# Score matmuls issued one head pair ahead, and the gate product moved from GpSimd to VectorE, in a retention block with FFN on eight Trainium2 cores

## The reference

```python
xn = layernorm(x)
# retention, 16 heads of 64
Q, K, V = xn @ Wq + bq, xn @ Wk + bk, xn @ Wv + bv      # split in heads
retained = ((Q @ K.T) / 8 * mask) @ V                   # mask[i, j] = 0.99**(i-j) for i >= j, else 0
normed = layernorm(retained) * gamma + beta             # over all 1024 features
s = (normed * sigmoid(xn @ Wg + bg)) @ Wo + bo
# feed-forward, 4096 wide
g = silu(gelu(xn @ w1 + b1) @ w2 + b2)
out = x + s * g
```

## Time and profile before

| quantity | value |
|---|---|
| three timed runs | 1761.42, 1877.56, 1886.75 us (median 1877.56) |
| the profiled execution's own time | 1759.84 us |
| span of its slowest core (core 3) | 1758.1 us |
| spans of the eight cores | 1728.0 to 1758.1 us |
| TensorE matmul busy in the span | 1359.8 us (77%) |
| VectorE, ScalarE, GpSimd busy | 469.7, 285.6, 146.4 us |

### The profile page before, as it was taken

One profiled execution on the slowest core, in us unless ns is written; L12 is line 12 of the kernel. 1 busy time (PEld: TensorE's weight loads), 2 busy tenths in 40 slices (PEclk: granted clock), 3 DMA queues, 4 the chain that ended last, 5 costly groups with the idle time before them and its releaser, 6 DMA issues.

```text
span 1758.1 us, 21259 instructions; the slowest of 8 cores (1728.0 to 1758.1 us)
## 1 busy us (share of the span) xinstructions
PE 1359.8 (77%) x7594; PEld 713.8 (41%) x7594; DVE 469.7 (27%) x1196; ACT 285.6 (16%) x594; POOL 146.4 (8%) x144
## 2 busy tenths in 40 slices
PE   0499966876287776886877868866599999999994
PEld 0144323533134323443343233432356666666662
DVE  0774011334044234233442342334001100111011
ACT  0021210110010110202101102011212222222221
POOL 0000000001000101001000010011002211221122
PEclk9988776887569677697686787976789999999997
DMA  8331034999700000001000000024502102110120
GB/s 154 107 113 44 1 72 84 124 116 118 110 1 24 25 1 25 25 0 48 1 25 25 1 4 22 1 96 156 212 4 72 49 25 72 73 48 32 65 73 36
DMA packets 15901, 100.42 MB, mean 57 GB/s; under 512 B 3253, under 2 KB 3638, under 8 KB 11830
## 3 DMA queue, kind: packets, MB, share of 16 engines
q0 software_dynamic: 6144, 44.06, 14.4%
q1 hardware_dynamic: 9510, 46.62, 8.2%
q10 hardware_dynamic: 144, 8.39, 1.3%
HBM read 109.56 MB, written 33.55 MB: 81 GB/s over the span
## 4 chain that ended last, share of the span: by engine, by line
PE 68%; DVE 12%; DMA 8%; issue 6%; ACT 3%; POOL 2%; DVEq 1%; SPq 0%; ACTq 0%; POOLq 0%
PE pY L1065 13%; PE pH L1041 9%; PE pPJ L555 7%; PE pM L867 6%; PE pPJ L517 4%; PE pS L790 4%; PE pPJ L534 3%; PE pPJ L592 3%; DMA s_scr<-WB 3%; PE pRT L642 2%; PE pRT L656 2%; PE pM L895 2%; PE pLATE L714 2%; DVE WB L627 2%; DMA WB<-w2b 2%
## 5 line engine op out<-in xcount | busy, mean ns | idle before, releaser
L1065 PE MATMUL pY<-WB,hT 128*128 128x512 bf16 x1024 | 226.6, 382 | 16.7 <-DMA WB<-w2b 16.7
L1041 PE MATMUL pH<-xnT,WB 128*128 128x256 bf16 x2048 | 227.5, 273 | 11.7 <-ACT hT L1051 10.7
L1041 PEld LDWEIGHTS pH<-xnT,WB 128*128 128x128 bf16 x2048 | 199.1, 98 | 41.6 <-issue 17.0
L790 PE MATMUL pS<-WB 128*128 128x512 bf16 x256 | 106.8, 540 | 122.3 <-POOL WB L780 66.3
L1065 PEld LDWEIGHTS pY<-WB,hT 128*128 128x128 bf16 x1024 | 100.9, 99 | 136.5 <-issue 20.8
L1095 DVE SCALAR_TENSOR_TENSOR xg<-pY,xg 128x1024 f32<-128x1024 f32 x16 | 19.6, 1225 | 471.6 <-ACT xg L1092 429.6
L1051 ACT ACTIVATE hT<-pH,b1Ts 128x256 bf16<-128x256 f32 x256 | 99.4, 479 | 226.8 <-PE pH L1041 226.8
L555 PE MATMUL pPJ<-xnT,WB 128*128 128x256 bf16 x1024 | 117.9, 276 | 12.3 <-DVE WB L546 12.3
L555 PEld LDWEIGHTS pPJ<-xnT,WB 128*128 128x128 bf16 x1024 | 93.7, 99 | 38.2 <-issue 16.3
L790 PEld LDWEIGHTS pS<-WB 128*128 128x128 bf16 x256 | 28.1, 116 | 194.4 <-issue 187.4
L867 PE MATMUL pM<-WB 128*128 128x512 bf16 x384 | 103.8, 436 | 0.0
(11 more groups left out here) (135 smaller groups left out, 1387.0 us busy)
## 6 DMA issues: line engine op xcount, KB each, us to landing
xg<-xpre SPq DMA_DIRECT2D x12, 1024.0 KB, 6.2
xg<-xseg SPq DMA_DIRECT2D x8, 1024.0 KB, 5.8
w1b<-w POOLq DMA_DIRECT2D x1, 8192.0 KB, 105.1
w2b<-w POOLq DMA_DIRECT2D x1, 8192.0 KB, 180.5
s_scr<-WB POOLq DMA_DIRECT2D x16, 512.0 KB, 3.0
xg<-xseg SPq DMA_DIRECT2D x16, 512.0 KB, 4.8
sld<-s_scr SPq DMA_DIRECT2D x16, 512.0 KB, 3.4
out<-sld POOLq DMA_DIRECT2D x16, 512.0 KB, 3.0
```

The source lines that it names most:

```text
L790: A("tensor", lambda e, it=it, dt=dt, ns=ns: e.matmul(pS[:, :], AsS[:, GRP * dt + 128 * it:GRP * dt + 128 * it + 128], WoS(1024 * dt + 512 ...
L1041: A("tensor", lambda e, dht=dht, dm=dm, sub=sub, pH=pH, gc=gc: e.matmul(pH[:, 256 * sub:256 * sub + 256], w1S(4096 * dm + 128 * dht, 128), ...
L1065: A("tensor", lambda e, lt=lt, dht=dht, ns=ns, it=it, pY=pY, half=half: e.matmul(pY[:, 512 * ns:512 * ns + 512], hT[:, 256 * lt + 128 * it ...
```

## The change

In `stageM2` the loop body is split in two functions. `m2_jb(hp)` issues the score matmuls and masks of a pair, `m2_ret(hp)` the matmuls that use them, the copy of `pRT` and the state's update. They are called as `m2_jb(0)`, and then for each pair `m2_jb(hp+1)` ahead of `m2_ret(hp)`. As two pairs' masked scores are alive at a time, the odd pairs get four tiles of their own, which lie in `xnb`; each mask of an odd pair also writes the token `b.xnb`, and each matmul on it reads that token. In `stageL` the product with the gate is issued on VectorE.

```diff
-                for hp in range(NP):
+                PmO = [xnb[:, 0:256], xnb[:, 256:512],
+                       xnb[:, 512:640], xnb[:, 640:768]]
+
+                def m2_jb(hp):
                     if hp % 2 == 0:
                         jb0b, jb0t = pSCB, "p.SCB"
                         jb1b, jb1t, jb1c = pSCA, "p.SCA", 256
+                        pm, pmt, extw = Pm, "b.Pm", []
                     else:
                         jb0b, jb0t = pLATE, "p.LATE"
                         jb1b, jb1t, jb1c = pS, "p.S", 0
+                        pm, pmt, extw = PmO, "b.PmX", ["b.xnb"]
...
-                          reads=[jb0t, "c.mask"], writes=["b.Pm0%d" % hh])
...
+                          reads=[jb0t, "c.mask"],
+                          writes=["%s0%d" % (pmt, hh)] + extw)
...
+                def m2_ret(hp):
+                    pm, pmt = (Pm, "b.Pm") if hp % 2 == 0 else (PmO, "b.PmX")
+                    extr = [] if hp % 2 == 0 else ["b.xnb"]
...
-                          reads=["b.V", "b.Pm0%d" % hh], writes=["p.RT"])
...
+                          reads=["b.V", "%s0%d" % (pmt, hh)] + extr,
+                          writes=["p.RT"])
...
+                m2_jb(0)
+                for hp in range(NP):
+                    if hp + 1 < NP:
+                        m2_jb(hp + 1)
+                    m2_ret(hp)
...
-                    A("gpsimd", lambda e, dt=dt, tA_=tA_: e.tensor_tensor(
+                    A("vector", lambda e, dt=dt, tA_=tA_: e.tensor_tensor(
                         AsS[:, GRP * dt:GRP * dt + GRP], tA_[:, :],
                         GtS[:, GRP * dt:GRP * dt + GRP], ALU.mult),
```

More of the change, by code:

```diff
@@ L626, in stageM2 @@
                           reads=["b.Ks", "b.Qs"], writes=[jb1t])
-                        A("vector", lambda e, hh=hh, jb0ap=jb0ap: e.tensor_tensor(
-                            Pm[hh][:, 0:256], jb0ap, maskS[:, 0:256],
+                        A("vector", lambda e, hh=hh, jb0ap=jb0ap, pm=pm: e.tensor_tensor(
+                            pm[hh][:, 0:256], jb0ap, maskS[:, 0:256],
                             ALU.mult),
-                          reads=[jb0t, "c.mask"], writes=["b.Pm0%d" % hh])
-                        A("vector", lambda e, hh=hh, jb1ap=jb1ap: e.tensor_tensor(
-                            Pm[2 + hh][:, 0:128], jb1ap, maskS[:, 0:128],
+                          reads=[jb0t, "c.mask"],
+                          writes=["%s0%d" % (pmt, hh)] + extw)
+                        A("vector", lambda e, hh=hh, jb1ap=jb1ap, pm=pm: e.tensor_tensor(
+                            pm[2 + hh][:, 0:128], jb1ap, maskS[:, 0:128],
                             ALU.mult),
[L634 to L638, removed]
+                          reads=[jb1t, "c.mask"],
+                          writes=["%s1%d" % (pmt, hh)] + extw)
+                def m2_ret(hp):
+                    pm, pmt = (Pm, "b.Pm") if hp % 2 == 0 else (PmO, "b.PmX")
+                    extr = [] if hp % 2 == 0 else ["b.xnb"]
                     for hh in range(2):
@@ L641, in stageM2 @@
                         ro = 64 * hh
[L642 removed]
+                        A("tensor", lambda e, h=h, ro=ro, hh=hh, pm=pm: e.matmul(
                             pRT[ro:ro + 64, 0:256] if ro == 0 else pRT[64:128, 0:256],
                             VS[:, 64 * h:64 * h + 64],
[L645 removed]
+                            pm[hh][:, 0:256],
                             start=True, stop=False, skip_group_check=True,
                             tile_position=(0, ro)),
[L648 to L649 removed]
+                          reads=["b.V", "%s0%d" % (pmt, hh)] + extr,
+                          writes=["p.RT"])
+                        A("tensor", lambda e, h=h, ro=ro, hh=hh, pm=pm: e.matmul(
                             pRT[ro:ro + 64, 128:256] if ro == 0 else pRT[64:128, 128:256],
                             VS[:, 1024 + 64 * h:1024 + 64 * h + 64],
[L652 removed]
+                            pm[2 + hh][:, 0:128],
                             start=False, stop=False, skip_group_check=True,
                             tile_position=(0, ro)),
[L655 removed]
+                          reads=["b.V", "%s1%d" % (pmt, hh)] + extr,
+                          writes=["p.RT"])
                         A("tensor", lambda e, h=h, ro=ro, hp=hp: e.matmul(
@@ L669, in stageM2 @@
                         for it in range(2):
-                            A("tensor", lambda e, h=h, ro=ro, it=it, hp=hp, g=g: e.matmul(
+                            A("tensor", lambda e, h=h, ro=ro, it=it, hp=hp: e.matmul(
                                 pSU[ro:ro + 64, 64 * hp:64 * hp + 64] if ro == 0
@@ L677, in stageM2 @@
                               reads=["b.Ku", "b.V"], writes=["p.SU"])
+                m2_jb(0)
[3 more added lines that the diff above has]
+                    m2_ret(hp)
+                if dbg and g == 0:
+                    A("sync", lambda e: e.dma_start(
+                        out=d_Pm[:, :], in_=Pm[0][:, 0:256]),
+                      reads=["b.Pm00"], writes=["d.out"], dma=True)
                 A("vector", lambda e: e.scalar_tensor_tensor(
```

## The result

| quantity | before | after |
|---|---|---|
| median of ten runs each | 1762.19 us (1756.65 to 1890.03) | 1787.58 us (1769.47 to 1865.47) |
| the profiled execution's own time | 1759.84 us | 1783.96 us |
| span of its slowest core (core 3) | 1758.1 us | 1782.4 us |
| spans of the eight cores | 1728.0 to 1758.1 us | 1758.7 to 1782.4 us |

The ratio of after to before is 1.0143, with the interval 1.0107 to 1.0179: about 25 us slower, and under the 2% line. With no change in the program some runs of either kernel lie 4 to 7% above the rest, four of the ten of before (1844 to 1890 us, two of them among the three runs shown ahead of the prediction) and two of the ten of after, and the ratio leaves these out.

What follows compares the result with a forecast made beforehand. TensorE's waits bound it: in stageL for VectorE's chain, in stageM2 for a mask. 22.5 + 3.1 = 25.6 us more gives 1785 us at the profiled level, 1903.2 us at the median's; range 1768 to 1925 us.

Steps and rivals of the forecast that it cites:

- The level: Whole kernel: 25.6 us added to the three timed runs' median of 1877.56 us, giving 1903.2 us.
- The sum: Whole kernel: 22.5 us from stageL plus 3.1 us from stageM2, 25.6 us more on 1759.84 us.
- Part 1: StageL's product on VectorE: a tile takes 1.92 us instead of 1.39, costing 22.5 us over groups 1 to 7.
- Part 2: StageM2's scores one pair ahead: 5.3 us lost less 2.2 us saved, net +3.1 us.
- The term of the odd pairs: StageM2: token b.xnb delays the second mask of each odd pair by 0.19 us, 5.3 us in all.
- The full-clock saving: StageM2 at full clock: the second head's matmuls no longer wait for masks, 0.23 us a pair, 2.2 us saved.
- Group 0's cover: Group 0's stageL: ScalarE's copy waits 36.71 us for a store behind the w2b transfer, absorbing all that group loses.
- Rival 1: StageM2: the other pair fills the second head's score wait, gaining 32.8 us; total -12.5 us, 1747 us; chance 5%.
- Rival 2: StageL: GpSimd sets the pace and the product gets cheaper, 0.42 for 0.72 us; about 1760 us; chance 6%.
- Rival 3: VectorE operations never overlap, 0.53 us apart throughout; stageL 4.6 us more a group, +30 us, 1790 us; chance 10%.
- Rival 4: Gate projection after stageL's longer pass: clock returns later, 25 us more, together +51 us, 1811 us; chance 12%.

Runs made afterwards that it cites:

- the first experiment: Product on VectorE alone, on the kernel before: 1762.73 us, ratio 1.0127 (1.0059 to 1.0194).
- the fastest kernel: Against the kernel before: scores ahead, token per tile, bank per head, interleaved product on VectorE, retained matmuls alternating between heads: 1632.3 us, ratio 0.9333.

## Why the prediction was near in the sum and wrong in the time

**The level (wrong).** The prediction says: "Both parts are stretches of waiting between engines, so I add the same sum to the median: 1877.56 + 25.6 = 1903.2 us." This is the step that failed. The sum was made against the profiled execution at 1759.84 us, and 1785 us is what came (1783.96 profiled, 1787.58 as a median). Three runs, of which two lay 6% up, were taken as the centre of the kernel's time, though the profiled execution and one of the three stood together at 1760. The median of ten runs is 1762.19. The range held both levels and so held the result.

**The sum (near, by offsets).** +25.6 us against +25 by the medians and +24.1 between the profiled executions.

- *Part 1, 22.5 us.* The path was right. The distances 0.53, 0.53, 0.53, 0.33 came as 0.53, 0.53, 0.51, 0.35, and the tile as 1.91 instead of 1.92 us. The stretch came as 15.61 us on average (15.50 to 15.85), for 15.60 in the sum. StageL as a whole lost 27.3 us: 109.3 - 86.1 = 23.2 in that stretch, 3.1 in the passes behind it, whose length depends on when the clock rises, and 1.0 around the broadcasts. In group 5 two of the three later passes ran at full clock before (1.89 us each from the first start to the last end, 3.57 at half clock), and after it was one. The product alone agrees, with 193 us of stageL for 164 and a total some 22 us longer.
- *Part 2, +3.1 us.* The term of the odd pairs was right: 3.52 against 3.34 us, and 6 us less once the shared token was gone, for 5.3 in the sum. Three of the four odd pairs stand inside the loop and the fourth at its start. What was missed is the rest of the start (0.68 us a group less that fourth 0.2) and the end (0.39), together about 6 us. I costed a pair in the steady state and never walked the first and the last one. The full-clock saving of 2.2 us didn't show: the full-clock time at the start of the stage now goes into the longer wait there. This part cost 11.8 us, not 3.1, so the size of this term was wrong too, by more than the sum shows.
- *Offsets.* StageS and stageM1 gave back 10.8 us, and the head start of core 3 in phase 0 another 3.3. StageS holds the same instructions, and in group 4 it took 13.40 us at a mean clock of 0.70 before and 11.90 us at 0.87 after. These are the two stretches, of before and then of after, in the columns of the earlier trace rows. It isn't a property of the new order: with the product alone, core 1 has 91.7 us of stageS and core 5 86.0. In stageM1 it is one stretch at half clock fewer in group 6 (41.75 to 39.64 us) and two fewer in group 7 (39.73 to 36.42), less 0.8 us in group 1. I had no term for this, and no run here shows what sets it. So that +24.1 us came so near to +25.6 is in good part luck: without these offsets the two parts cost 39 us on this core, of which the sum had two thirds.

```profile
859.40:872.80 13.40, 11.11 (x37) 3.31 (x33) 6.47 (x21) 3.21 (x9) 0.00 (x0) 0.70 0.01 1
```

```profile
871.40:883.30 11.90, 8.73 (x37) 2.89 (x34) 6.41 (x21) 3.18 (x9) 0.00 (x0) 0.87 0.01 2
```

- *Group 0's cover (right).* w2b took as long as before (180.3 us after its issue, 180.5 before), and the store's wait shrank. That the transfer is fixed held to 3 us only, since its issue moved.

**The rivals.** Rival 1, the overlap, needs the wait ahead of L620 gone; it is 39.9 us, and it goes when each head has a bank of its own. Then the order brings 46 us in the pairs (161 to 115, a part of it by the clock), more than the 32.8 us that I gave the wait. Rival 2, that GpSimd sets the pace, fell with the first experiment. Rival 3 (0.53 us throughout) fell with the 0.35 and 0.33 us in the rows. Of what the Trainium skill says in "VectorE: DVE Perf Modes", section "The DRAIN you can't avoid", the statement that a semaphore costs nothing extra doesn't hold here: the wait did cost 0.2 us for each operation. The other one, that the next operation doesn't start until the pipe is empty, the prediction cited without its limit: the same section adds that an operation which isn't held starts earlier, and the 0.33 us agree with that. Rival 4, a later clock, didn't come; the gate projection took 7.10 us at 1.00 in group 3, and sums to 50.4 us against 50.8.

## What to carry to other kernels

Work out an operation's cost by whether it waits for the one just ahead on its engine: moved onto a chain, a faster operation can cost more than a slower one on an idle engine, and interleaving two chains takes the cost away. When work is issued ahead to fill a wait, check in the engine's order that it stands in front of the waiting instruction; if it doesn't, find what the wait protects (here a bank shared by two heads), and walk the loop's first and last round as well as its middle. Add the sum to the level at which it was made, and don't take the median of three scattered runs for the kernel's time.

## What the hardware showed that I had not expected

- Score matmuls of two heads, on 64 rows each, started 0.01 us apart once they wrote different banks. The second head's L622 even started (579.03) ahead of the first head's L628 (579.21), which stands before it in the list. The prediction's "TensorE takes its instructions in order" held for the waits and not for every start. Matmuls on 64 columns each ran side by side even into one bank's two halves of partitions (both L651 in 0.52 us, one alone in 0.42). A pair of heads went from 3.34 us to 2.30 and 1.59 at the same granted clock of 0.50.
- Less waiting came with more clock: the mean granted clock of the cores was 0.825 to 0.845 before and 0.876 to 0.891 in the fastest kernel, and a pair at full clock takes 1.31 us there.
- The same stage with the same instructions differed by 6.6% between two cores of one execution (91.7 and 86.0 us of stageS), by the moment at which the clock rose alone as far as the rows show. Differences of 5 us in a total of 1750 can't be read as the work of an edit without the stage sums.
- VectorE waited 0.71 us for GpSimd to finish reading a tile; with four tiles in place of two the same pass went from 10.64 to 7.17 us.
